# GpSimd makes its score products in four pieces, with output scatters between them

## The chip, the cores and the metric

The program runs on one core of one Trainium2 chip. The core has engines that run their own instruction streams and meet only at semaphores: TensorE (PE, matmuls), VectorE (DVE, elementwise work and reductions), ScalarE (ACT, activations and copies), GpSimd (POOL, elementwise work and the indirect DMAs that scatter rows), and SyncE (SP), which issues most other DMAs. The metric is the device time of one execution in microseconds (us), as the median of the runs taken.

## The reference

Two transformer layers on x of 32 batches x 256 tokens x 128 channels, float32. Cut to what is computed:

```python
x = L0_attn_x                       # (32, 256, 128)
xn = layernorm(x)
x = x + attn0(xn) + moe0(xn)
xn = layernorm(x)
x = x + conv1(xn) + moe1(xn)

# attn0: 16 heads of width 8; attention runs over the HEADS of one token, not over the tokens
q = xn @ Wq + bq ; kv = (xn @ Wdown + bdown) @ Wup + bup ; q, k = rope(q), rope(k)
att = softmax(einsum('bthd,btgd->bthg', q, k) / sqrt(8))     # a 16x16 matrix per token
out = einsum('bthg,btgd->bthd', att, v) @ Wout + bout

# moe0, moe1: 8 experts of width 512, each token takes its best 2 (GELU between two matmuls)
# conv1: layernorm, projection to 3 x 128, two causal convolutions of 128 taps, gates, projection
```

The rotation of q and k is the same for all heads of a token and cancels in the product of a token's own q and k; the kernel leaves it out of the arithmetic.

## The kernel before

The 8192 tokens are 64 tiles of 128 tokens, one token per partition. Attention takes them in 32 pairs, `NPAIR`. Since a token attends only over its own heads, the scores are no matmul: for each pair, somebody multiplies q (broadcast over the key heads) with k (broadcast over the query heads), 2 tiles x 16 x 16 x 8 = 4096 products per partition, and a reduction adds each group of 8. Then the softmax over 16, a second product with v, a second reduction, and a division.

VectorE does this in a loop over the pairs b. `scores(b)` makes or awaits the products, reduces them (L983), takes the maximum (L985) and subtracts it (L986). `weighted(b - 1)` then sums the exponentials of the pair before (L995), multiplies them with v in four instructions (L1000), takes reciprocals (L1007), reduces (L1009) and scales (L1012); `add_heads(b - 3)` adds a finished projection to x (L991). For pairs 0 to 10, VectorE makes the products itself (`own_product`). From pair `OWN` = 11 on, GpSimd makes them (L257, called from its own program), one tile of the pair per instruction, into one of two buffers.

Alongside, from step `T_FIRST` = 10 on, the first layer's experts run: 71 tiles of 256 rows sorted by expert, three in each step. TensorE computes a tile's hidden layer (L678) and output (L691), ScalarE applies the GELU (L486) and evacuates the row indices (L494) and the output (L495), and GpSimd scatters the output to DRAM by row index, two indirect DMAs per tile (L427, `scatter_outputs`). The output buffers are four: ScalarE's evacuation of tile f waits until the scatter of tile f - 4 has landed. ScalarE also evacuates the q, k and v of coming pairs (L501) and takes the exponentials (L510).

The order of the work is written out by hand: every engine walks the same step number b, and counts on semaphores hold the steps together. The ones around the change are:

- `s_on` (heads_ready): VectorE's L1012 of a pair is done. GpSimd waits for it before the first product of a pair: at step b, which makes pair b + 1, for pair b - 2.
- `s_pv` (values_weighted): the fourth L1000 is done. GpSimd waits for it before the second product: at step b, for the L1000 that VectorE runs in its own iteration b.
- `s_qkv` (qkv_ready): q, k and v of the pair are in SBUF.
- `s_pp` (pool_product_halves): counts up by two for each pair; VectorE's L983 of the pair waits for both.
- `s_yev` (expert_out_ready): ScalarE has evacuated a tile; its scatter waits for it. GpSimd scatters three tiles behind (`late`).

Of the kernel before, what the change touches and what calls it, by code (L numbers as in the profile page):

```python
# [8 lines left out]
H, DH = 16, 8  # L9
# [27 lines left out]
NPAIR = NT // 2  # L37
# [6 lines left out]
def tiles_of(b):  # L44

    f0 = PER_STEP * (b - T_FIRST)
    return [f for f in range(max(f0, 0), min(f0 + PER_STEP, NF))] if b >= T_FIRST else []
# [5 lines left out]
def mixed_layers(nc, x, consts, w128, w32, rows, moe0, bout0, moe1, bout1, kpad0, kpad1, out):  # L53
# [5 lines left out]
    with ctx:  # L59
# [3 lines left out]
        def sem(name):  # L63
            return ctx.enter_context(nc.semaphore(name))
# [145 lines left out]
        s_pp = sem("pool_product_halves")  # L210
# [36 lines left out]
        def wait(eng, s, n):  # L247

            if n > 0:
                eng.wait_ge(s, n)  # L250

        def qk_product(eng, b, t, h0=0, n=H):

            q = qkv[:, b % 4, t, h0 * DH:(h0 + n) * DH].rearrange("p (h e) -> p h e", h=n)
            k = qkv[:, b % 4, t, D:2 * D].rearrange("p (g e) -> p g e", g=H)
            o = t * 2048 + h0 * D
            return eng.tensor_tensor(  # L257
                prod[:, b % 2, o:o + n * D].rearrange("p (h g e) -> p h g e", h=n, g=H),
                q[:, :, None, :].to_broadcast([P, n, H, DH]), k[:, None, :, :].to_broadcast([P, n, H, DH]), ALU.mult)
# [116 lines left out]
        @block.gpsimd  # L376
        def _(pool):
            psteps = [0]

            def plink(ins):  # L380
                psteps[0] += 1
                ins.then_inc(s_pst, 1)
                pool.wait_ge(s_pst, psteps[0])

            def in_three_parts(dst, src, n):
                m1 = cst[0:3, C_M1:C_M1 + 1].to_broadcast([3, n])
                m2 = cst[0:3, C_M2:C_M2 + 1].to_broadcast([3, n])
                plink(pool.tensor_copy(partb[:, 0:n], src))
                plink(pool.tensor_tensor(parts[:, 0:n], partb[:, 0:n], m1, ALU.mult))
                plink(pool.tensor_tensor(part[:, 0:n], parts[:, 0:n], src, ALU.add))  # L390
                plink(pool.tensor_copy(partb[:, 0:n], part[:, 0:n]))
                plink(pool.tensor_tensor(parts[:, 0:n], partb[:, 0:n], m2, ALU.mult))
                plink(pool.tensor_tensor(part[:, 0:n], parts[:, 0:n], part[:, 0:n], ALU.add))
                plink(pool.tensor_copy(dst, part[:, 0:n]))

            plink(pool.memset(pat, 0.0))
            pool.iota(patr[:, :, D].bitcast(u32), [[1, FILL]], base=2 * TOKS, channel_multiplier=FILL).then_inc(s_pat, 1)
            for k in range(2):
                pool.iota(tags[:, k, :], [[2, NT]], base=k, channel_multiplier=2 * NT)
            pool.wait_ge(s_cst, 48)  # L400
            pool.wait_ge(s_set, 1)
            pool.wait_ge(s_brow, 1)
            in_three_parts(b3[0:3, :], brow, B_END)
            pool.sem_inc(s_b3, 1)
            pool.wait_ge(s_bf, 32)
            for layer in range(2):
                in_three_parts(bout3[:, layer, :], boutf[:, layer, :], E * D)
            for layer in range(2):
                pool.dma_start(bo3_d[layer], bout3[:, layer, :]).then_inc(s_bo3st, 16)
            pool.sem_inc(s_bo3, 1)  # L410

            def scatter(layer):
                pool.wait_ge(s_rows, layer + 1)
                pool.wait_ge(s_zf[layer], 16 * NFILL)
                for k in range(2):
                    wait(pool, s_sc, 16 * NT * (2 * layer + k))
                    plink(pool.tensor_copy(XN[:, :, D].bitcast(u32), tags[:, k, :]))  # L417
                    for j in range(NT):
                        pool.indirect_dma_start(  # L419
                            sorted_x[layer], bass.IndirectOffsetOnAxis(ap=idx[:, k, j:j + 1], axis=0),  # L420
                            XN[:, j, :], None).then_inc(s_sc, 16)

            def scatter_outputs(layer, f):
                G = layer * NF + f
                pool.wait_ge(s_yev, G + 1)
                for r in range(FR):
                    pool.indirect_dma_start(  # L427
                        y_d[layer], bass.IndirectOffsetOnAxis(ap=yidx[:, G % 4, r:r + 1], axis=0),
                        ys[:, G % 4, r * D:(r + 1) * D], None).then_inc(s_ysc[G % 4], 16)

            scatter(0)
            for b in range(OWN - 1, LAST_STEP + 1):
                late = [f - 3 for f in tiles_of(b) if f >= 3]
                if b + 1 < NPAIR:
                    pool.wait_ge(s_qkv, 2 * (b + 1) + 2)
                    pool.wait_ge(s_on, b - 1)
                    qk_product(pool, b + 1, 0).then_inc(s_pp, 1)
                for f in late[:2]:
                    scatter_outputs(0, f)
                if b + 1 < NPAIR:  # L440
                    pool.wait_ge(s_pv, b)
                    qk_product(pool, b + 1, 1).then_inc(s_pp, 1)
                for f in late[2:]:
                    scatter_outputs(0, f)
            for f in range(NF - 3, NF):
                scatter_outputs(0, f)

            scatter(1)
            for f in range(NF):
                scatter_outputs(1, f)  # L450
# [730 lines left out]
```

## Time and profile before

| | |
|---|---|
| median of 3 runs | 1376.99 us (1376.89 to 1383.17) |
| profiled execution, its own time | 1375.78 us |
| its span | 1373.8 us |
| PE busy | 958.8 us, 70% of the span, 6400 matmuls |
| DVE busy | 860.7 us, 63%, 1144 instructions |
| ACT busy | 602.6 us, 44% |
| POOL busy | 812.7 us, 59%, 617 instructions |
| POOL L257, score products | x42, 189.8 us, mean 4519 ns |
| POOL L427, output scatters, both layers | x284, 309.9 us, mean 1091 ns |
| mean granted TensorE clock | 0.877 |

No engine is busy for the whole span, since the stages have different limits: VectorE's attention to about 310 us, a stage from there to about 735 us in which the rest of attention and the first experts run together, then combination, projection and convolution, and the second experts from about 1035 us. The change touches the stage from 314 to 700 us only. In a chain or a timeline a row gives the start in us from the start of the span, the duration in us, the engine and the line of the program.

### The profile page before, as it was taken

How to read it: one execution, taken by the hardware profiler on the slowest of the kernel's cores; microseconds unless marked ns; L12 is line 12 of the kernel's file. 1: busy time of each engine (PE TensorE's matmuls, PEld its weight loads, DVE VectorE, ACT ScalarE, POOL GpSimd, SP SyncE). 2: the span in 40 equal slices, each digit the busy share in tenths (PEclk: the TensorE clock that was granted, in tenths of full speed). 3: DMA queues.
4: the chain of work that ended last, by engine and by line, in shares of the span. 5: the costliest groups of instructions: out<-in, count | busy, mean ns of one | idle time of the engine just before them, and what ended most of it. 6: DMA issues, size and time to landing. Idle time of an engine off the chain costs nothing.

```text
span 1373.8 us, 19050 instructions
## 1 busy us (share of the span) xinstructions
PE 958.8 (70%) x6400; PEld 843.1 (61%) x6400; DVE 860.7 (63%) x1144; ACT 602.6 (44%) x1533; POOL 812.7 (59%) x617
## 2 busy tenths in 40 slices
PE   1442222217988888887872458889978999999975
PEld 1431011106877776676772457789977999998864
DVE  7949999999999999999995986111122000000028
ACT  0120000005765665565664448900005566665567
POOL 4604877776999999999971003767643445544420
PEclk9995555558999999999996789999998999999988
DMA  5472323313544444544454420189995777777647
GB/s 173 160 294 92 112 79 112 109 42 86 172 131 141 135 138 140 145 132 136 131 160 197 153 93 24 54 277 318 306 355 153 202 201 205 205 206 200 196 186 214
DMA packets 119953, 225.60 MB, mean 164 GB/s; under 512 B 16709, under 2 KB 80101, under 8 KB 117810
## 3 DMA queue, kind: packets, MB, share of 16 engines
q1 hardware_dynamic: 102164, 188.16, 44.9%
q0 software_dynamic: 17344, 35.57, 7.1%
q8 instruction: 52, 0.85, 0.3%
q10 hardware_dynamic: 350, 0.67, 0.2%
q14 instruction: 43, 0.35, 0.1%
HBM read 157.19 MB, written 67.14 MB: 163 GB/s over the span
## 4 chain that ended last, share of the span: by engine, by line
DVE 32%; PE 29%; POOL 15%; DMA 12%; ACT 6%; issue 5%; SPq 1%; POOLq 0%; ACTq 0%; DVEq 0%
PE ps L691 9%; PE ps L678 9%; POOL BG L257 9%; POOL y_tok L427 7%; DVE BG L983 5%; DVE BG L1009 5%; DVE BG L1000 5%; DMA FF<-sorted_x 4%; DMA TPB<-in_kpad 4%; DVE BG L257 3%; DVE XN L880 3%; PE ps L790 2%; PE ps L792 2%; DVE stats L850 2%; PE ps L669 1%
## 5 line engine op out<-in xcount | busy, mean ns | idle before, releaser
L427 POOL DMA_INDIRECT y_tok<-FF,yidx x284 | 309.9, 1091 | 212.4 <-ACT FF L495 154.9
L419 POOL DMA_INDIRECT sorted_x<-XN,idx x256 | 274.4, 1072 | 87.1 <-issue 85.7
L678 PE MATMUL ps<-FF 128*128 128x256 f32 x1136 | 283.9, 395 | 0.0
L691 PE MATMUL ps<-FF 128*128 128x128 f32 x2272 | 280.2, 277 | 0.0
L691 PEld LDWEIGHTS ps<-FF 128*128 128x128 f32 x2272 | 268.7, 194 | 16.8 <-issue 6.3
L486 ACT ACTIVATE FF<-ps,FF 128x256 f32<-128x256 f32 x568 | 230.4, 479 | 37.1 <-PE ps L678 36.5
L678 PEld LDWEIGHTS ps<-FF 128*128 128x128 f32 x1136 | 214.6, 199 | 25.5
L257 POOL TENSOR_TENSOR BG<-TPB 128x2048 f32<-128x2048 f32 x42 | 189.8, 4519 | 11.1 <-DVE BG L1000 6.8
L1127 DVE TENSOR_TENSOR BG<-BG,ps 128x512 f32<-128x512 f32 x16 | 10.6, 686 | 291.3 <-PE ps L824 291.0
L1000 DVE TENSOR_TENSOR BG<-BG,TPB 128x1024 f32<-128x1024 f32 x128 | 147.8, 1214 | 0.0
L983 DVE TENSOR_REDUCE BG<-BG 128x512 f32<-128x4096 f32 x32 | 141.2, 4411 | 0.4
L1009 DVE TENSOR_REDUCE BG<-BG 128x256 f32<-128x4096 f32 x32 | 139.5, 4358 | 0.0
L478 ACT COPY FF<-ps 128x256 f32<-128x256 f32 x142 | 54.2, 382 | 162.0 <-PE ps L669 161.7
L494 ACT COPY yidx<-FF 128x2 uint32<-128x2 uint32 x142 | 27.9, 196 | 221.6 <-PE ps L691 116.8
L417 POOL COPY XN<-tags 128x64 uint32<-128x64 uint32 x4 | 1.2, 298 | 176.4 <-DVEq L962 170.4
L651 PE MATMUL ps<-cst,XN 128*128 128x128 f32 x128 | 24.9, 331 | 89.2 <-DVE XN L880 89.2
L669 PE MATMUL ps<-cst,FF 128*128 128x128 f32 x284 | 56.4, 281 | 43.0 <-DMA FF<-sorted_x 41.4
L719 PE MATMUL ps<-b,ones 128*128 128x384 bf16 x64 | 24.2, 379 | 84.9 <-ACT BG L506 58.5
L790 PE MATMUL ps<-BG,TPB 128*128 128x128 f32 (+1 forms) x352 | 73.0, 289 | 8.9 <-DMA TPB<-in_kpad 7.1
L651 PEld LDWEIGHTS ps<-cst,XN 128*128 128x128 f32 x128 | 19.0, 174 | 91.9 <-DVE XN L880 69.3
L501 ACT COPY TPB<-ps 128x384 f32<-128x384 f32 x64 | 30.8, 481 | 96.7 <-PE ps L720 62.0
L719 PEld LDWEIGHTS ps<-b,ones 128*128 128x128 bf16 x64 | 6.6, 104 | 98.3 <-issue 65.5
(180 smaller groups left out, 1676.8 us busy)
## 6 DMA issues: line engine op xcount, KB each, us to landing
FF<-in_moe SPq DMA_DIRECT2D x142, 514.0 KB
TPB<-in_kpad SPq DMA_DIRECT2D x22, 1024.0 KB, 7.9
sorted_x<-TPB SPq DMA_DIRECT2D x36, 516.0 KB, 4.1
FF<-sorted_x SPq DMA_DIRECT2D x142, 129.0 KB
FF<-in_kpad SPq DMA_DIRECT2D x10, 1024.0 KB, 8.0
BG<-y_tok SPq DMA_DIRECT2D x8, 1024.0 KB, 6.6
X<-y_tok SPq DMA_DIRECT2D x8, 1024.0 KB, 5.9
y_tok<-FF,yidx POOLq DMA_INDIRECT x284, 3.3
```

Of the source, the lines that this page charges most:

```text
L257: return eng.tensor_tensor(prod[:, b % 2, o:o + n * D].rearrange("p (h g e) -> p h g e", h=n, g=H), q[:, :, None, :].to_broadcast([P, n, H ...
L419: pool.indirect_dma_start(sorted_x[layer], bass.IndirectOffsetOnAxis(ap=idx[:, k, j:j + 1], axis=0), XN[:, j, :], None).then_inc(s_sc, 16)
L427: pool.indirect_dma_start(y_d[layer], bass.IndirectOffsetOnAxis(ap=yidx[:, G % 4, r:r + 1], axis=0), ys[:, G % 4, r * D:(r + 1) * D], None ...
L478: act.copy(xsT[:, G % 2, :], psT[:, 0:FT]).then_inc(s_xsT, 1)
L486: g = act.activation(hT[:, G % 2, m, :], psH[2 * (G % 2) + m // 2][:, (m % 2) * FT:(m % 2 + 1) * FT], ACT.Gelu, bias=wc[:, G % 4, HID + MK ...
L669: t = pe.transpose(psT[:, r * P:(r + 1) * P], xs[:, G % 4, r, 0:D], ident)
L678: t = pe.matmul(psH[2 * (G % 2) + m // 2][:, (m % 2) * FT:(m % 2 + 1) * FT], wc[:, G % 4, m * P:(m + 1) * P], xsT[:, G % 2, :], start=True ...
L691: t = pe.matmul(psY[:, r * P:(r + 1) * P], hT[:, G % 2, m, r * P:(r + 1) * P], wc[:, G % 4, HID + m * D:HID + (m + 1) * D], start=False, s ...
L790: pe.matmul(bank[:, k * NT:k * NT + n0], tp[N % 3][:, k, diag:diag + P], V[:, col:col + n0], start=True, stop=False)
L983: link(dve.tensor_reduce(S[:, b % 2, :], prod[:, b % 2, :].rearrange("p (n d) -> p n d", d=DH), AX.X, ALU.add))
L1000: i = dve.tensor_tensor(prodv[:, o:o + n * D].rearrange("p (h e g) -> p h e g", h=n, e=DH), S[:, b % 2, so:so + n * H].rearrange("p (h g) ...
L1009: reduced = mark(dve.tensor_reduce(O, prodv.rearrange("p (n g) -> p n g", g=H), AX.X, ALU.add))
```

## The change

GpSimd's products for a pair were two instructions, each on all 16 query heads of one tile (2048 products per partition). They become four, each on eight query heads (1024 products per partition), through the arguments `h0` and `n` that `qk_product` already has. The step's three tiles of output scatters were placed two after the first product and one after the second. Now one stands after each of the first three pieces, and the fourth piece comes last. The waits stay: `s_qkv` and `s_on` ahead of the first piece, `s_pv` ahead of the third. `s_pp` is counted up at the second and the fourth piece.

```diff
             for b in range(OWN - 1, LAST_STEP + 1):
                 late = [f - 3 for f in tiles_of(b) if f >= 3]
-                if b + 1 < NPAIR:
+                made = b + 1 < NPAIR
+                if made:
                     pool.wait_ge(s_qkv, 2 * (b + 1) + 2)
                     pool.wait_ge(s_on, b - 1)
-                    qk_product(pool, b + 1, 0).then_inc(s_pp, 1)
-                for f in late[:2]:
+                    qk_product(pool, b + 1, 0, 0, H // 2)
+                for f in late[:1]:
                     scatter_outputs(0, f)
-                if b + 1 < NPAIR:
+                if made:
+                    qk_product(pool, b + 1, 0, H // 2, H // 2).then_inc(s_pp, 1)
+                for f in late[1:2]:
+                    scatter_outputs(0, f)
+                if made:
                     pool.wait_ge(s_pv, b)
-                    qk_product(pool, b + 1, 1).then_inc(s_pp, 1)
+                    qk_product(pool, b + 1, 1, 0, H // 2)
                 for f in late[2:]:
                     scatter_outputs(0, f)
+                if made:
+                    qk_product(pool, b + 1, 1, H // 2, H // 2).then_inc(s_pp, 1)
```

GpSimd's queue in step 12, before. L257 are the products (`BG` holds them, `TPB` holds q and k), L427 the scatters, two to a tile:

```order
L257 TENSOR_TENSOR BG<-TPB 128x2048 [waits heads_ready,qkv_ready]
L427 DMA y_tok<-FF,yidx 17408x128 [waits expert_out_ready]
L427 DMA y_tok<-FF,yidx 17408x128
L427 DMA y_tok<-FF,yidx 17408x128 [waits expert_out_ready]
L427 DMA y_tok<-FF,yidx 17408x128
L257 TENSOR_TENSOR BG<-TPB 128x2048 [waits values_weighted]
L427 DMA y_tok<-FF,yidx 17408x128 [waits expert_out_ready]
L427 DMA y_tok<-FF,yidx 17408x128
```

The same step of the changed kernel:

```order
L257 TENSOR_TENSOR BG<-TPB 128x1024 [waits heads_ready,qkv_ready]
L427 DMA y_tok<-FF,yidx 17408x128 [waits expert_out_ready]
L427 DMA y_tok<-FF,yidx 17408x128
L257 TENSOR_TENSOR BG<-TPB 128x1024
L427 DMA y_tok<-FF,yidx 17408x128 [waits expert_out_ready]
L427 DMA y_tok<-FF,yidx 17408x128
L257 TENSOR_TENSOR BG<-TPB 128x1024 [waits values_weighted]
L427 DMA y_tok<-FF,yidx 17408x128 [waits expert_out_ready]
L427 DMA y_tok<-FF,yidx 17408x128
L257 TENSOR_TENSOR BG<-TPB 128x1024
```

The third tile's scatters stood behind all products of the step; they now stand ahead of the last piece. The second tile's scatters still stand behind the whole of the first tile's products, and the first tile's behind only half of them. VectorE's queue is the same in both kernels; one iteration of it, for reference:

```order
L983 TENSOR_REDUCE BG<-BG 128x512 [waits pool_product_halves]
L985 TENSOR_REDUCE BG<-BG 128x32 [waits vector_step]
L986 TENSOR_TENSOR BG<-BG 128x512 [waits vector_step]
L995 TENSOR_REDUCE BG<-BG 128x32 [waits probs_ready]
L1000 TENSOR_TENSOR BG<-BG,TPB 128x1024 x4
L1007 RECIPROCAL BG<-BG 128x32 [waits vector_step]
L1009 TENSOR_REDUCE BG<-BG 128x256 [waits values_weighted]
L1012 TENSOR_TENSOR BG<-BG 128x256 [waits heads_transposed,vector_step]
L991 TENSOR_TENSOR X<-X,ps 128x256 [waits attention_out_psum]
```

Nothing moved here; the wait of L983 is for the second and the fourth piece now.

## Rows read from the trace of the kernel before

**Rows 1.** Chain that ended last, window 381 to 400 us, shares by line

```profile
by line: POOL BG L257 71.4%; POOL y_tok L427 40.4%; issue 12.8%
```

**Rows 2.** Timeline of POOL, same window; start us, us, instruction, idle before it

```profile
381.14 4.53 POOL L257 TENSOR_TENSOR BG<-TPB 128x2048 f32<-128x2048 f32 x1
385.84 1.00 POOL L427 DMA_INDIRECT y_tok<-FF,yidx  x1 [0.17 <-issue]
...
388.13 4.51 POOL L257 TENSOR_TENSOR BG<-TPB 128x2048 f32<-128x2048 f32 x1
392.81 1.27 POOL L427 DMA_INDIRECT y_tok<-FF,yidx  x1 [0.17 <-issue]
394.39 1.39 POOL L427 DMA_INDIRECT y_tok<-FF,yidx  x1 [0.30 <-issue]
396.08 1.96 POOL L427 DMA_INDIRECT y_tok<-FF,yidx  x1 [0.30 <-issue]
...
399.33 4.53 POOL L257 TENSOR_TENSOR BG<-TPB 128x2048 f32<-128x2048 f32 x1
```

**Rows 3.** Busy time by stretch: start:end, length, engines, PEclk, DMA share, GB/s

```profile
344.78:526.51 181.73, 153.58 (x968) 131.97 (x967) 180.69 (x121) 113.14 (x278) 165.75 (x81) 0.95 0.49 142
690.00:735.00 45.00, 33.89 (x240) 30.08 (x239) 32.51 (x26) 24.76 (x66) 29.71 (x25) 1.00 0.43 128
```

**Rows 4.** Timeline of DVE, window 381 to 400 us

```profile
384.73 1.23 DVE L1012 TENSOR_TENSOR BG<-BG 128x256 f32<-128x256 f32 x1
...
386.22 4.41 DVE L983 TENSOR_REDUCE BG<-BG 128x512 f32<-128x4096 f32 x1
...
391.38 1.82 DVE L986 TENSOR_TENSOR BG<-BG 128x512 f32<-128x512 f32 x1
393.13 0.67 DVE L995 TENSOR_REDUCE BG<-BG 128x32 f32<-128x512 f32 x1
393.72 4.61 DVE L1000 TENSOR_TENSOR BG<-BG,TPB 128x1024 f32<-128x1024 f32 x4
398.26 0.34 DVE L1007 RECIPROCAL BG<-BG 128x32 f32<-128x32 f32 x1
```

**Rows 5.** Timeline of DVE, 300 to 320 us, POOL not multiplying beside these

```profile
304.65 0.35 DVE L1007 RECIPROCAL BG<-BG 128x32 f32<-128x32 f32 x1
...
309.31 0.42 DVE L1012 TENSOR_TENSOR BG<-BG 128x256 f32<-128x256 f32 x1
...
309.99 4.63 DVE L257 TENSOR_TENSOR BG<-TPB 128x1024 f32<-128x1024 f32 x4
...
319.82 0.69 DVE L986 TENSOR_TENSOR BG<-BG 128x512 f32<-128x512 f32 x1
```

**Rows 6.** Groups by line, POOL: xcount, busy us, mean ns, idle before

```profile
L393 POOL TENSOR_TENSOR BG<-BG 3x1024 f32<-3x1024 f32 x3 | 7.0, 2328 | 0.2
```

**Rows 7.** Timeline of ACT, window 391 to 398 us

```profile
397.26 0.19 ACT L494 COPY yidx<-FF 128x2 uint32<-128x2 uint32 x1 [3.41 <-DMA y_tok<-FF,yidx]
```

**Rows 8.** Timeline of POOL, window 300 to 352 us

```profile
325.73 4.54 POOL L257 TENSOR_TENSOR BG<-TPB 128x2048 f32<-128x2048 f32 x1 [6.78 <-DVE BG L1000]
333.58 4.53 POOL L257 TENSOR_TENSOR BG<-TPB 128x2048 f32<-128x2048 f32 x1 [3.31 <-ACT TPB L501]
```

**Rows 9.** Timeline of DVE, iterations 10, 11, 30 and 31

```profile
325.56 0.35 DVE L1007 RECIPROCAL BG<-BG 128x32 f32<-128x32 f32 x1
...
343.71 0.34 DVE L1007 RECIPROCAL BG<-BG 128x32 f32<-128x32 f32 x1
...
688.93 0.34 DVE L1007 RECIPROCAL BG<-BG 128x32 f32<-128x32 f32 x1
...
695.05 4.41 DVE L983 TENSOR_REDUCE BG<-BG 128x512 f32<-128x4096 f32 x1
```

**Rows 10.** Chain that ended last, window 710 to 716 us

```profile
711.04 0.34 DVE X L991
...
711.52 0.27 PE ps L707
```

## The prediction

> **What bounds the kernel now.** I read the chain of waits first. In the stage that the change touches it alternates between GpSimd's products (L257) and scatters (L427); in one step of it nothing else appears [rows 1]. So I read GpSimd's timeline of that step next. It is closed: product, two scatters, product, four scatters, product, and every gap is 0.02 to 0.30 us with "issue" as its cause [rows 2]. The step from 381.14 to 399.33 takes 18.19 us; the ten steps from 344.78 to 526.51 take 181.73, or 18.17 each [rows 3]. The reader is to see that GpSimd waits for no other engine there.
>
> VectorE's timeline of the same step comes next [rows 4]. It has no gap either (180.69 us busy of 181.73 [rows 3]), but not all of it is work. L986 takes 1.82 us where it takes 0.69 with no product beside it, and L1012 takes 1.23 against 0.42 [rows 4, 5]. The product that started at 388.13 ends at 392.64 and L995 follows the stretched L986 at 393.13, 0.49 later [rows 2, 4]. L983, a reduction with one input, runs beside the same product in 4.41 us and is not held. In the other direction, the scatters that meet the four L1000 take 1.27, 1.39 and 1.96 us against 1.00 [rows 2]. VectorE free of this needs, from one L1007 to the next: 5.34 to the next pair's first instruction (304.65 to 309.99 [rows 5]), 5.16 from L983 to L986, 0.61 for L986 (its 0.69 less the 0.08 by which L995 overlaps it), 0.59 from L995 to L1000, and 4.54 to L1007 [rows 4]: 16.24 us. The engines hold each other up, and 18.17 is GpSimd's sum.
>
> The Trainium skill, page "SBUF — State Buffer", section "SBUF: two separate sides", says that VectorE and GpSimd share a port pair as an exclusive lock, for an operation with two SBUF inputs against a GpSimd operation that reads SBUF, and that whoever starts first keeps it for the whole instruction. The trace agrees: 1.82 against 0.69.
>
> **The change, part by part.** *The pieces.* GpSimd's elements stay the same. The trace has no piece of 1024 such elements. Half of 4.52 is 2.26, which is the lower end; GpSimd's own product of two 1024-element inputs took 2.328 [rows 6], though on three partitions. I take 2.33. For the upper end I add the 0.17 us that GpSimd needs to go from a product to a scatter: 2.50. Queueing a tile's scatters behind a piece costs 2.46 when VectorE reduces (385.67 to 388.13) and 3.14 when it multiplies (392.64 to 395.78) [rows 2].
>
> *The scatters between.* What matters is the wait for `s_pv`, which stands ahead of the third piece as it stood ahead of the second product. Before, it cost nothing: that product started at 399.33, while L1007 had started at 398.26, and a product that really waited started 0.17 after L1007's start (325.56 to 325.73) [rows 8, 9]. So it had 0.90 us in hand. After the wait came one whole product, 4.53, and then VectorE's next L983 could go. Now after the wait come a piece, a tile's scatters, and a piece. I follow one step from L1007's start, calling the pieces 1 to 4:
>
> - Piece 3 starts at 0.17 and ends at 2.50.
> - The third tile's scatters run beside L1009, a reduction: 2.46, to 4.96.
> - Piece 4 wants to start at 4.96. L1012 started at 4.66 (304.65 to 309.31 [rows 5]) and lasts 0.42; I let the piece start at 5.02. It ends at 7.35.
> - VectorE would have reached L983 at 5.34. It waits until 7.45, two microseconds that were not there before (0.10 of them for the signal, an estimate from the 0.17 above, which also held the last L1000's end).
> - Piece 1 of the next step finds `s_on` counted up by the L1012 just named, so it follows at 7.37 and ends at 9.70.
> - The first tile's scatters, beside L983: to 12.16.
> - Piece 2 starts at 12.16. L986 is ready at 7.45 + 5.16 = 12.61, 0.45 too late, and is held until piece 2 ends at 14.49.
> - L995 follows at 14.98 and L1000 at 15.57; L1007 at 20.11.
> - The second tile's scatters, 3.14, end at 17.6 under the L1000 instructions. GpSimd then waits 2.6 us for `s_pv`.
>
> The step is 20.11 us against 18.17: plus 1.94. All four pieces and two tiles' scatters are now in series with L986 to L1000. One tile's scatters have cover and GpSimd pays its own wait instead. What was saved, the scatter that took 1.96 beside L1000, lies in that wait and is worth nothing.
>
> The order of events hardly depends on the 0.45. If L986 got in first at 12.61, piece 2 would follow at 13.2 and end at 15.6, L1000 would wait for it instead of L986, and L1007 would come at 20.2.
>
> *Other queues.* The waits for the scatters' landing are on ScalarE (L494 [rows 7]), 3.41 us there. The first and third tiles' scatters now come earlier in the step relative to VectorE, so these waits shrink. TensorE and ScalarE gain slack and decide nothing. GpSimd's wait for `s_qkv` cost 3.31 once, at 333.58 [rows 8], and never again. Would TensorE's clock fall when a step has 10% more idle time? From 690 to 735 us TensorE was 75% busy and granted 1.00, against 85% and 0.95 in the ten steps [rows 3], so no.
>
> *The sum.* Step 11 starts at 333.58 as before: its first two pieces and two tiles' scatters, 4.66 + 6.28, end at 344.5. Waiting for a running L1000 adds 0.6, so piece 3 starts at 345.1. L1007 of iteration 12 comes at 345.1 + 19.94 = 365.0, against 343.71 + 18.17 = 361.9. Eighteen more steps bring iteration 30 to 365.0 + 18 x 20.11 = 727.0, against 688.93 [rows 9]: 38.1 late. L983 of pair 31 follows 7.45 later, at 734.4 against 695.05: 39.4 late. No products follow. The stage's end hangs on VectorE's L1012 and L991, which release TensorE's last matmuls (L991 at 711.04, L707 at 711.52 [rows 10]), so nothing of the 39.4 is given back, and the later stages shift whole. On the profiled execution's own time, 1375.78 us, this gives 1415.2; that execution lies 1.2 us under the median, which I leave. For pieces of 2.26 the step is 0.28 shorter, times 19 or so: 1410. For 2.50 it is 0.68 longer: 1428.
>
> The Trainium skill, page "GPSIMD Engine Reference", section "3.1 Elementwise — side-by-side cycle accounting", gives about 2.6 cycles for each element of a two-input operation, and the page's clock is 1.2 GHz. By it a piece would be estimated at 2.22 us, the step at 19.67 and the time at 1407. No trace row of this case has the piece itself, so the row of 2.328 decides.
>
> **The rivals.** *Faster: the wait does not bind, and GpSimd stays the bound.* Its own sum would be 4 x 2.33 + 2 x 2.46 + 3.14 + 0.04 = 17.4 against 18.17, over 20 steps -15 us: 1361. For it: GpSimd is the closed chain now [rows 1, 2]. Against it: the wait is in the queue with 0.90 us in hand, and L1000 would have to come 2.7 us earlier than the pieces allow.
>
> *No change: the lock does not bite at L986.* Then VectorE sets the step: 7.45 + 5.16 + 0.61 + 0.59 + 4.54 = 18.35, plus 0.18. Over 19 steps that is 3.4, with 2 us for step 11 and the end: 1381. Against it: in each of the ten steps a product that overlaps L986 stretched it. For it: the overlap hangs on times that my sum gives to within half a microsecond, and some scatters may fall otherwise.
>
> *Much slower: piece 2 loses to L986 and is not let in between the L1000 instructions.* It would start when L1007 does, at 18.35, end at 20.7, and the second tile's scatters would take it to 23.1 before piece 3: a step of 23.0, +4.9 over 20 steps, 1473. It decides from the point where scatters or pieces run 0.45 us longer than I have them. Against it: the scatters of before got in at the ends of single L1000 instructions (the one at 394.39 finished at 395.78, well inside the four [rows 2, 4]), and L995, with one input, leaves a gap first.
>
> **How the numbers follow.** The forecast, 1415 with its own range of 1407 to 1432, has 0.80. The faster rival has 0.08, no change 0.06, much slower 0.06. Together the rivals are the two in ten that the range leaves out; below it I allow for a lock that bites in part of the steps, above it for pieces at 2.50 and an ill-placed scatter: 1397 to 1436. A difference under 0.5%, 6.9 us, could not be told from none. Faster by more than that 0.08, within it 0.06, slower 0.86.
>
> **What would show it.** In the changed kernel's profile: pieces of 2.33 us, steps of 20.1 us on GpSimd's timeline; a wait of 2.6 us ahead of every third piece, released by L1000; a gap of about 2 us on VectorE ahead of L983, released by L257; L986 still stretched, to about 2.5 us; L1012 back at 0.42. The stage from 690 us on should look as before, 39 us later. I am wrong if GpSimd's timeline stays closed, if L983 starts 5.34 after L1007, or if L986 takes 0.69.

## The result and the profile after

The changed kernel is slower: 1428.15 us median of 4 runs (1426.69 to 1428.73) against 1377.41 us (1376.89 to 1383.17) for the kernel before, a ratio of 1.0357 with a 95% interval of 1.0328 to 1.0386. The profiled execution took 1428.73 us, its span is 1426.8 us. A second set of runs gave 1.0313 (1.0295 to 1.0332).

In the changed file VectorE's lines stand seven further down: L983 is L990, L986 is L993, L995 is L1002, L1000 is L1007, L1007 is L1014, L1009 is L1016, L1012 is L1019, L991 is L998. Scatters keep L427 and products L257. From the page of the changed kernel, the chain by engine, the two groups of GpSimd and the reduction of VectorE that awaits the products (line, engine, operation, count, busy us, mean ns, idle before and its releaser):

```profile
DVE 54%; PE 28%; DMA 9%; ACT 4%; issue 2%; POOL 2%; SPq 1%; POOLq 0%; ACTq 0%; DVEq 0%
...
L427 POOL DMA_INDIRECT y_tok<-FF,yidx x284 | 291.2, 1025 | 218.0 <-ACT FF L502 163.8
...
L257 POOL TENSOR_TENSOR BG<-TPB 128x1024 f32<-128x1024 f32 x84 | 197.2, 2349 | 69.0 <-DVE BG L1007 57.0
...
L990 DVE TENSOR_REDUCE BG<-BG 128x512 f32<-128x4096 f32 x32 | 141.2, 4411 | 3.3 <-POOL BG L257 2.9
```

A piece takes 2.349 us. The scatters did get cheaper: 1025 ns on average where they took 1091. But GpSimd now idles 69 us ahead of the products, 57 of them for the fourth L1007, and the chain has left it for VectorE. The prediction had expected VectorE to wait some 2 us ahead of L990 in every step; over the whole kernel it waits 2.9 us there for GpSimd. One step on GpSimd's timeline, which answers to [rows 2]:

```profile
405.92 2.35 POOL L257 TENSOR_TENSOR BG<-TPB 128x1024 f32<-128x1024 f32 x1 [2.66 <-DVE BG L1007]
408.43 1.00 POOL L427 DMA_INDIRECT y_tok<-FF,yidx  x1 [0.16 <-issue]
409.74 0.96 POOL L427 DMA_INDIRECT y_tok<-FF,yidx  x1 [0.30 <-issue]
410.72 2.34 POOL L257 TENSOR_TENSOR BG<-TPB 128x1024 f32<-128x1024 f32 x1
413.50 2.34 POOL L257 TENSOR_TENSOR BG<-TPB 128x1024 f32<-128x1024 f32 x1 [0.44 <-DVE BG L1019]
415.99 1.00 POOL L427 DMA_INDIRECT y_tok<-FF,yidx  x1 [0.16 <-issue]
417.30 0.96 POOL L427 DMA_INDIRECT y_tok<-FF,yidx  x1 [0.30 <-issue]
418.29 2.35 POOL L257 TENSOR_TENSOR BG<-TPB 128x1024 f32<-128x1024 f32 x1
420.80 1.27 POOL L427 DMA_INDIRECT y_tok<-FF,yidx  x1 [0.17 <-issue]
422.38 1.39 POOL L427 DMA_INDIRECT y_tok<-FF,yidx  x1 [0.30 <-issue]
```

The third piece waits 2.66 us for the values; one tile's scatters follow, the fourth piece, and after a new wait of 0.44 us the next step's first piece. VectorE over the same step, which answers to [rows 4]:

```profile
405.76 0.34 DVE L1014 RECIPROCAL BG<-BG 128x32 f32<-128x32 f32 x1
406.02 4.36 DVE L1016 TENSOR_REDUCE BG<-BG 128x256 f32<-128x4096 f32 x1
410.41 2.94 DVE L1019 TENSOR_TENSOR BG<-BG 128x256 f32<-128x256 f32 x1
413.27 0.41 DVE L998 TENSOR_TENSOR X<-X,ps 128x256 f32<-128x256 f32 x1
413.61 4.41 DVE L990 TENSOR_REDUCE BG<-BG 128x512 f32<-128x4096 f32 x1
418.05 0.69 DVE L992 TENSOR_REDUCE BG<-BG 128x32 f32<-128x512 f32 x1
418.77 2.43 DVE L993 TENSOR_TENSOR BG<-BG 128x512 f32<-128x512 f32 x1
421.12 0.67 DVE L1002 TENSOR_REDUCE BG<-BG 128x32 f32<-128x512 f32 x1
421.71 4.61 DVE L1007 TENSOR_TENSOR BG<-BG,TPB 128x1024 f32<-128x1024 f32 x4
426.25 0.34 DVE L1014 RECIPROCAL BG<-BG 128x32 f32<-128x32 f32 x1
```

The step is 20.49 us (405.76 to 426.25). VectorE shows no gap. It is late inside two instructions: L1019 takes 2.94 us where it needs 0.42, and L993 takes 2.43 where it needs 0.69 [rows 5]. Both end shortly after a piece of GpSimd does (pieces end at 413.06 and 420.64). In the steady steps, which are like this one, about 4.25 of the 20.49 us are time in which an instruction of VectorE is recorded as running and is held. The stretch of 18 steps and the end of the stage, as busy time by stretch (same columns as [rows 3]):

```profile
364.73:733.65 368.92, 283.91 (x1710) 246.67 (x1710) 367.05 (x217) 199.69 (x488) 287.46 (x180) 0.92 0.41 123
...
738.00:783.00 45.00, 33.25 (x220) 30.49 (x220) 30.95 (x26) 18.58 (x51) 25.30 (x24) 0.88 0.36 108
```

The steps are 368.92 / 18 = 20.50 us each. TensorE was granted 0.92 in them and 0.88 in the end of the stage; [rows 3] has 0.95 and 1.00.

### The profile page after: what moved, and what is told of

Read it like the earlier page. It is cut to its first block, busy times and chain, and to the rows that moved or that the text cites. A ratio compares the mean times of both kernels' runs of the same rounds, so it can differ in the third digit from the quotient of the medians.

```text
span 1426.8 us, 19092 instructions
## 1 busy us (share of the span) xinstructions
PE 976.5 (68%) x6400; PEld 864.8 (61%) x6400; DVE 904.5 (63%) x1144; ACT 601.7 (42%) x1533; POOL 801.5 (56%) x659
## 4 chain that ended last, share of the span: by engine, by line
DVE 54%; PE 28%; DMA 9%; ACT 4%; issue 2%; POOL 2%; SPq 1%; POOLq 0%; ACTq 0%; DVEq 0%
DVE BG L1007 9%; DVE BG L990 9%; DVE BG L1016 9%; PE ps L698 9%; PE ps L685 9%; DVE BG L1019 4%; DVE BG L993 4%; DVE BG L257 3%; PE ps L797 3%; DVE XN L887 3%; DMA FF<-sorted_x 3%; DMA TPB<-in_kpad 2%; PE ps L799 2%; DVE stats L857 2%; DVE BG L992 1%
## 5 line engine op out<-in xcount | busy, mean ns | idle before, releaser
L427 POOL DMA_INDIRECT y_tok<-FF,yidx x284 | 291.2, 1025 | 218.0 <-ACT FF L502 163.8
L698 PEld LDWEIGHTS ps<-FF 128*128 128x128 f32 x2272 | 284.7, 204 | 17.1 <-issue 4.5
L698 PE MATMUL ps<-FF 128*128 128x128 f32 x2272 | 294.7, 286 | 0.0
L685 PE MATMUL ps<-FF 128*128 128x256 f32 x1136 | 271.6, 382 | 0.0
L257 POOL TENSOR_TENSOR BG<-TPB 128x1024 f32<-128x1024 f32 x84 | 197.2, 2349 | 69.0 <-DVE BG L1007 57.0
L685 PEld LDWEIGHTS ps<-FF 128*128 128x128 f32 x1136 | 206.9, 192 | 22.7
L1007 DVE TENSOR_TENSOR BG<-BG,TPB 128x1024 f32<-128x1024 f32 x128 | 149.9, 1231 | 0.0
L990 DVE TENSOR_REDUCE BG<-BG 128x512 f32<-128x4096 f32 x32 | 141.2, 4411 | 3.3 <-POOL BG L257 2.9
L1016 DVE TENSOR_REDUCE BG<-BG 128x256 f32<-128x4096 f32 x32 | 139.5, 4358 | 0.0
L714 PE MATMUL ps<-b,ones 128*128 128x256 bf16 x32 | 11.4, 355 | 128.4 <-DVE X L998 127.8
L714 PEld LDWEIGHTS ps<-b,ones 128*128 128x128 bf16 x32 | 3.3, 104 | 147.1 <-issue 145.9
L658 PEld LDWEIGHTS ps<-cst,XN 128*128 128x128 f32 x128 | 20.5, 185 | 88.3 <-DVE XN L887 65.6
```

What stands on the lines that cost most here:

```text
L257: return eng.tensor_tensor(prod[:, b % 2, o:o + n * D].rearrange("p (h g e) -> p h g e", h=n, g=H), q[:, :, None, :].to_broadcast([P, n, H ...
L427: pool.indirect_dma_start(y_d[layer], bass.IndirectOffsetOnAxis(ap=yidx[:, G % 4, r:r + 1], axis=0), ys[:, G % 4, r * D:(r + 1) * D], None ...
L685: t = pe.matmul(psH[2 * (G % 2) + m // 2][:, (m % 2) * FT:(m % 2 + 1) * FT], wc[:, G % 4, m * P:(m + 1) * P], xsT[:, G % 2, :], start=True ...
L698: t = pe.matmul(psY[:, r * P:(r + 1) * P], hT[:, G % 2, m, r * P:(r + 1) * P], wc[:, G % 4, HID + m * D:HID + (m + 1) * D], start=False, s ...
L990: link(dve.tensor_reduce(S[:, b % 2, :], prod[:, b % 2, :].rearrange("p (n d) -> p n d", d=DH), AX.X, ALU.add))
L1007: i = dve.tensor_tensor(prodv[:, o:o + n * D].rearrange("p (h e g) -> p h e g", h=n, e=DH), S[:, b % 2, so:so + n * H].rearrange("p (h g) ...
```

## The experiments

The columns of the comparison are the same throughout: the median and the ratio to the kernel before on the same chip with its 95% interval; the step, from one reciprocal of VectorE to the next in the profile; and by how much VectorE's two-input instructions ran over what they take alone, the subtraction (L986 before) first and the scaling of the heads (L1012) or the products with the values (L1000) second. Edits of a "changed" or "split" kernel and of the one with the old order are shown against the changed kernel, the others against the kernel before.

| kernel | median us | ratio, 95% | step us | VectorE held, us in a step |
|---|---|---|---|---|
| before | 1377.4 | 1 | 18.17 | 1.13 + 0.80 |
| changed | 1428.2 | 1.0357 (1.0328 to 1.0386) | 20.49 | 1.74 + 2.51 |
| pieces, old order | 1383.0 | 1.0037 (1.0019 to 1.0054) | 18.46 | 1.28 + 0.94 |
| second tile split | 1392.2 | 1.0115 (1.0090 to 1.0139) | 18.77 | 2.52, scaling |
| first tile split | 1391.7 | 1.0113 (1.0089 to 1.0137) | 18.83 | 2.59, value products |
| changed, no values wait | 1422.1 | 1.0336 (1.0310 to 1.0363) | 20.13 | 1.74 + 2.15 |
| changed, piece 4 after heads | 1419.7 | 1.0318 (1.0294 to 1.0342) | 20.21 | 1.77, and a wait of 2.12 |
| before, no values wait | 1376.0 | 1.0000 (0.9984 to 1.0016) | 18.17 | 1.13 + 0.80 |
| before, VectorE takes 4 heads | 1357.1 | 0.9877 (0.9842 to 0.9912) | 17.10 | 0.08 + 0.05 |
| before, VectorE takes 5 heads | 1356.5 | 0.9838 (0.9820 to 0.9856) | 17.14 | 0.04 |
| before, VectorE takes 6 heads | 1361.7 | 0.9902 (0.9868 to 0.9935) | 17.28 | 0.05 |
| changed, again | 1422.6 | 1.0313 (1.0295 to 1.0332) | 20.49 | as changed |

The last column accounts for the one before it. VectorE's own work in a step was 16.24 us in the prediction's sum. Adding what held it gives 16.24 + 1.93 = 18.17, 16.24 + 4.25 = 20.49, 16.24 + 2.22 = 18.46, + 2.52 = 18.76, + 2.59 = 18.83, + 3.89 = 20.13. For piece 4 after the heads it gives 16.24 + 1.77 + 2.12 = 20.13, 0.08 short of the step. This is bookkeeping: it must come out for any engine without gaps, and says where the time is, not why. The reasons come from the single runs.

**Pieces without a new order.** Four pieces, scatters where they stood.

```diff
                     qk_product(pool, b + 1, 0, 0, H // 2)
-                for f in late[:1]:
-                    scatter_outputs(0, f)
-                if made:
                     qk_product(pool, b + 1, 0, H // 2, H // 2).then_inc(s_pp, 1)
-                for f in late[1:2]:
+                for f in late[:2]:
                     scatter_outputs(0, f)
                 if made:
                     pool.wait_ge(s_pv, b)
                     qk_product(pool, b + 1, 1, 0, H // 2)
+                    qk_product(pool, b + 1, 1, H // 2, H // 2).then_inc(s_pp, 1)
                 for f in late[2:]:
                     scatter_outputs(0, f)
-                if made:
-                    qk_product(pool, b + 1, 1, H // 2, H // 2).then_inc(s_pp, 1)
```

> Four pieces of eight heads, but each pair of pieces back to back and all scatters where they stood before. My theory: what costs is the scatters between pieces that the next VectorE reduction waits for, not the number of pieces. Then only the two extra instructions count: 4 x 2.35 against 9.04 us, step 18.17 + 0.36 = 18.5 us, and 19 steps of it 7 us: 1384. Rival, the pieces themselves cost it (dispatch, a further lock for each): step 20.5 us and 1428.

Measured 1383.0 us and a step of 18.46. The number of pieces costs 0.29 us a step. That is their surplus: in this run the two pairs of pieces take 4.67 and 4.65 us, together 9.32, where the two whole products take 9.04 [rows 2]. The rest of the loss, 20.49 less 18.46, is the order.

**Only the second tile split.** The first tile's product is whole, followed by two tiles' scatters; behind the wait come piece, scatters, piece.

```diff
                     pool.wait_ge(s_qkv, 2 * (b + 1) + 2)
                     pool.wait_ge(s_on, b - 1)
-                    qk_product(pool, b + 1, 0, 0, H // 2)
-                for f in late[:1]:
+                    qk_product(pool, b + 1, 0).then_inc(s_pp, 1)
+                for f in late[:2]:
                     scatter_outputs(0, f)
-                if made:
-                    qk_product(pool, b + 1, 0, H // 2, H // 2).then_inc(s_pp, 1)
-                for f in late[1:2]:
-                    scatter_outputs(0, f)
```

> Only the second tile's product is split, with the third tile's scatters between its two pieces; the first tile's product is whole and followed by two tiles of scatters. My theory: the path from the wait for the values is piece, scatters, piece, whole product, and GpSimd then still has four scatters beside L1000, 6.5 us: step 18.75 to 18.95 us, +0.7 x 19.5 = 14 us, 1391; VectorE's L1012 stretched to 2.9 us. Rival, this split alone is the whole cost (it alone lies between the wait and the reduction that needs it): step 20.5, 1428.

Measured 1392.2 us. VectorE's timeline (the reciprocal is L1010, the scaling of the heads L1015, the subtraction L989 here), and the two waits of GpSimd in that step:

```profile
400.50 0.34 DVE L1010 RECIPROCAL BG<-BG 128x32 f32<-128x32 f32 x1
...
405.16 2.96 DVE L1015 TENSOR_TENSOR BG<-BG 128x256 f32<-128x256 f32 x1
...
413.54 0.69 DVE L989 TENSOR_TENSOR BG<-BG 128x512 f32<-128x512 f32 x1
...
419.28 0.34 DVE L1010 RECIPROCAL BG<-BG 128x32 f32<-128x32 f32 x1
```

```profile
400.67 2.35 POOL L257 TENSOR_TENSOR BG<-TPB 128x1024 f32<-128x1024 f32 x1 [0.39 <-DVE BG L1003]
...
408.26 4.53 POOL L257 TENSOR_TENSOR BG<-TPB 128x2048 f32<-128x2048 f32 x1 [0.43 <-DVE BG L1015]
```

This step is 18.78. The whole hold is on the scaling, 2.96 us against the 2.9 forecast, and the subtraction is free. The size of the step came as forecast, but not quite by the path that the expectation names: GpSimd waits 0.39 us for the values and 0.43 for the heads, so its own queue does not set the step. VectorE does, with its own 16.24 us and the 2.5 by which piece, scatters and piece behind the wait for the values hold its scaling. The rival's 20.5 is excluded.

**Only the first tile split.**

```diff
                     pool.wait_ge(s_pv, b)
-                    qk_product(pool, b + 1, 1, 0, H // 2)
+                    qk_product(pool, b + 1, 1).then_inc(s_pp, 1)
                 for f in late[2:]:
                     scatter_outputs(0, f)
-                if made:
-                    qk_product(pool, b + 1, 1, H // 2, H // 2).then_inc(s_pp, 1)
```

> Only the first tile's product is split, with the first tile's scatters between its pieces and the second's behind; the second tile's product is whole, followed by the third tile's scatters. My theory: the path is 0.17 + 4.53 + 2.46 + 2.35 + 2.46 + 2.35 + 5.62 = 19.95 us, +1.8 x 19.5 = 35 us, 1412, with L986 (the subtraction) stretched by a late second piece. Rival, only the split of the second tile costs: step 18.2 to 18.5, 1377 to 1384.

Measured 1391.7 us, between the two theories, and both were wrong. Below are GpSimd's second piece, then VectorE's products with the values (L1005 here), all four and the first by itself:

```profile
412.67 2.35 POOL L257 TENSOR_TENSOR BG<-TPB 128x1024 f32<-128x1024 f32 x1
```

```profile
412.31 7.20 DVE L1005 TENSOR_TENSOR BG<-BG,TPB 128x1024 f32<-128x1024 f32 x4
```

```profile
412.31 3.80 DVE L1005 TENSOR_TENSOR BG<-BG,TPB 128x1024 f32<-128x1024 f32 x1
```

My path had the piece hold the subtraction. With the second product whole, the reduction of the products is not late, so the subtraction and the sum are through when piece 2 comes, and it holds the value products instead. The path is shorter by those two, 0.61 + 0.59: 19.95 - 1.20 = 18.75, measured 18.83.

So the two splits cost 0.60 and 0.66 us alone and 2.32 together. The missing 1.06 comes from the same pair of instructions: the split of the second tile makes VectorE late, and so moves the subtraction and the sum, 1.20 us, behind piece 2, which the split of the first tile has already made late. The 0.14 that this is too much is mostly that the second tile's split adds 0.49 us ahead of piece 1 here, and not 0.60: 7.58 against 7.09 us from the start of piece 3, or of the whole product, to the start of piece 1.

**The wait taken out.**

```diff
                 if made:
-                    pool.wait_ge(s_pv, b)
                     qk_product(pool, b + 1, 1, 0, H // 2)
```

> The changed kernel without GpSimd's wait for the fourth L1000 ahead of the third piece; its buffer is free by the wait for the heads. My theory: that wait puts four pieces and two tiles of scatters in series with L986 to L1000. Without it GpSimd need not stand 2.6 us idle per step and its own sum is 17.4 us; the pieces will now meet L1000, so I give the step 18.5 us, 1384 (between 17.4 and 19.5 us, 1362 to 1403). Rival, the port lock costs the same wherever the pieces fall, and the wait only hid it: step 20.5 or more, 1428 or more.

Measured 1422.1 us: my 1384 was wrong and the rival nearly right. VectorE (L992 is the subtraction, L1006 the value products), then GpSimd's third piece and the next step's first:

```profile
398.52 2.43 DVE L992 TENSOR_TENSOR BG<-BG 128x512 f32<-128x512 f32 x1
...
401.48 6.76 DVE L1006 TENSOR_TENSOR BG<-BG,TPB 128x1024 f32<-128x1024 f32 x4
```

```profile
403.55 2.47 POOL L257 TENSOR_TENSOR BG<-TPB 128x1024 f32<-128x1024 f32 x1
...
413.38 2.34 POOL L257 TENSOR_TENSOR BG<-TPB 128x1024 f32<-128x1024 f32 x1 [1.77 <-DVE BG L1018]
```

The third piece now cuts in among the value products and holds them for 2.15 us (6.76 against 4.61), where with the wait the fourth had held the scaling for 2.51. GpSimd's idle time moved to the wait for the heads, 1.77 us. The wait for the values is worth 0.36 us a step in the profile, not the 2 us that I had put on it; the time alone cannot be told from that of the changed kernel, since the intervals overlap.

**The fourth piece behind the heads.**

```diff
                 if made:
+                    pool.wait_ge(s_on, b)
                     qk_product(pool, b + 1, 1, H // 2, H // 2).then_inc(s_pp, 1)
```

> The changed kernel with one wait more: GpSimd's fourth piece waits for VectorE's scaling of the heads in the same iteration. In the changed kernel that scaling starts 0.31 us ahead of the fourth piece's recorded start and yet is held until the piece ends (2.94 us), which delays the next first piece and the next reduction. My theory: a product behind a scatter takes the port before its recorded start, so the order that the prediction assumed needs this wait; the scaling takes 0.42 again, the step falls from 20.49 to 20.2 us, the time by 19.5 x 0.3 = 6 us to 1422. Rival, something else holds the scaling or the wait costs as much as it saves: step 20.5 or more, 1428 or more.

Measured 1419.7 us (1.0318 against 1.0357 and 1.0313 for the changed kernel), step 20.21. The step agrees with the theory. The 6 us in the time are too few to tell from the changed kernel: the intervals overlap with both of its own. GpSimd, then VectorE:

```profile
410.25 4.64 POOL L257 TENSOR_TENSOR BG<-TPB 128x1024 f32<-128x1024 f32 x2 [0.23 <-DVE BG L1020]
```

```profile
409.75 0.42 DVE L1020 TENSOR_TENSOR BG<-BG 128x256 f32<-128x256 f32 x1
...
412.62 4.42 DVE L991 TENSOR_REDUCE BG<-BG 128x512 f32<-128x4096 f32 x1 [2.12 <-POOL BG L257]
```

This is the order that the prediction had assumed: scaling in 0.42 us, then piece 4 and the next piece 1 without a gap, and VectorE waiting 2.12 us in the open ahead of its reduction. The prediction gave this order a step of 20.11; the added wait keeps piece 4 back by 0.23 us.

**The wait taken out of the kernel before.**

```diff
                 if b + 1 < NPAIR:
-                    pool.wait_ge(s_pv, b)
                     qk_product(pool, b + 1, 1).then_inc(s_pp, 1)
```

> The kernel before, two whole products, without the wait for the values ahead of the second one. My theory: the wait was met 0.9 us before GpSimd came to it, so nothing changes: step 18.17 us, 1377. Rival, the wait sets the phase between the two engines and without it the second product drifts into the L1000 instructions: step above 18.5, above 1384.

Measured 1376.0 us, ratio 1.0000 (0.9984 to 1.0016), step 18.17. In the kernel before, that wait decides nothing once the steps are steady. The first three steps with GpSimd's products differ, 24.36, 16.24 and 17.06 us against 20.91, 18.15 and 18.18, and together they are only 0.4 us longer. The one of 16.24 (reciprocals at 328.17 and 344.40) is a step in which no product holds VectorE: the subtraction takes 0.69 and the scaling 0.43. It measures the sum of 16.24 that the prediction had put together.

**GpSimd relieved.** VectorE multiplies the last 4 (5, 6) query heads of the second tile.

```diff
                     pool.wait_ge(s_pv, b)
-                    qk_product(pool, b + 1, 1).then_inc(s_pp, 1)
+                    qk_product(pool, b + 1, 1, 0, H - 4).then_inc(s_pp, 1)
...
                 else:
+                    dve.wait_ge(s_qkv, 2 * b + 2)
+                    link(qk_product(dve, b, 1, H - 4, 4))
                     dve.wait_ge(s_pp, 2 * (b - OWN) + 2)
```

> The kernel before, with 4 of the 16 query heads of a pair's second tile multiplied by VectorE, just ahead of the reduction, and 12 left to GpSimd. My theory of the kernel before is that GpSimd's own sum is the step, so 1.1 us less of it shortens the step to 17.1 us while VectorE's sum, 16.24 + 0.62, stays under it: 1377.4 - 20 x 1.07 = 1356. Rival, VectorE is the bound that counts: step 18.17 + 0.6, 1389. Second rival, TensorE and ScalarE, which wait for the scatters, take over at 18 us: 1374.

> As the run with 4 heads on VectorE, with 6. GpSimd's sum falls by 1.7 us to 16.5, VectorE's rises to 16.24 + 0.91 = 17.15 and should now set the step, with little of it held by products: 17.2 us, 1377.4 - 20 x 0.97 = 1358. Rival, GpSimd's sum still sets it: 16.6 us, 1346. Second rival, VectorE is held by products as much as before: 19.1 us, 1396.

> The kernel before with 5 of the second tile's 16 query heads on VectorE. With 4 the step was GpSimd's closed sum, 17.10 us; with 6 it was VectorE's, 17.28. My theory: with 5, GpSimd's sum is 16.83 and VectorE's 16.24 + 0.80 + 0.05 = 17.09, so the step is 17.1 us and the time that of 4 heads, 1357. Rival, the two lock each other in a phase that neither 4 nor 6 has, L986 and L1012 both stretched: 17.6 us or more, 1366 or more.

Measured 1357.1, 1361.7 and 1356.5 us, steps 17.10, 17.28 and 17.14. With 4 heads on VectorE (L988 is the subtraction, L1014 the scaling) and GpSimd's shorter product:

```profile
405.09 0.77 DVE L988 TENSOR_TENSOR BG<-BG 128x512 f32<-128x512 f32 x1
...
415.57 0.47 DVE L1014 TENSOR_TENSOR BG<-BG 128x256 f32<-128x256 f32 x1
...
416.30 0.68 DVE L257 TENSOR_TENSOR BG<-TPB 128x512 f32<-128x512 f32 x1
```

```profile
411.98 3.44 POOL L257 TENSOR_TENSOR BG<-TPB 128x1536 f32<-128x1536 f32 x1
```

The times of all three came within 4 us of their forecasts, and GpSimd's sum is confirmed as what set the step before. VectorE got more work and its step became shorter, since the products now come earlier against it. The shorter one ends at 415.42, before the scaling starts; the whole one ends at 405.31, 0.22 after the subtraction's start. Of the 1.93 us of hold 0.13 is left. These versions are faster than both kernels, by 1.0 to 1.6% against the one before.

**The changed kernel again.**

> The changed kernel once more, unaltered. In its first profile the stages between the first combination and the second layer's experts took 308.8 us, where the eight profiles of the kernel before and its variants other than this one took 300 to 304. My theory: nothing there belongs to the change, and TensorE's granted clock in the convolution (0.96 against 1.00) made the difference in that execution; a second profile shows 300 to 304 again, steps of 20.49 us and a time near 1424. Rival, the later start of that stage brings the lower clock each time: 308 again, 1428.

Measured 1422.6 us on a chip where the kernel before took 1378.5, steps of 20.49 again. The convolution's stretch in the first profile and in this one:

```profile
950.00:1078.00 128.00, 117.75 (x993) 116.56 (x992) 22.13 (x32) 0.00 (x0) 78.84 (x83) 0.96 0.94 306
```

```profile
950.00:1078.00 128.00, 114.15 (x995) 112.32 (x994) 22.14 (x32) 0.00 (x0) 78.99 (x84) 0.99 0.98 321
```

From the first combination to the second layer's experts this profile took 302.8 us, not 308.8. The surplus of the first profile is not a constant part of the change. Whether the lower granted clock (0.96) or the slower transfers (306 against 321 GB/s) made it, these runs do not separate.

## Why the prediction was right, and where its sizes were off

The direction held, and in the steady steps the chain of instructions that the prediction followed ran as it said but for one place. The time was 1428 where 1415 was forecast, inside the range. The profiled executions differ by 52.95 us, and 39.4 were forecast. The prediction's upper case, pieces of 2.50 us, also gives 1428; that is chance, for the pieces took 2.35 and other terms made the difference. What the prediction had wrong is the share of the single parts in the loss.

- *GpSimd's closed sum bounds the kernel before.* Right: 1.1 us less of GpSimd's work took 1.07 us off the step.
- *The pieces.* Taken at 2.33, measured 2.349 on average; in the step shown the four take 9.38 where 9.32 was assumed. The estimate of 2.22 from the page "GPSIMD Engine Reference" of the Trainium skill (section 3.1) was too low by 0.13; the row of the three-partition product was the better guide.
- *The wait for the values costs 2.6 us of GpSimd's time, and one tile's scatters have cover.* Right as described: 2.66. As a cause I made too much of it: "what matters is the wait", says the prediction, and without it the step is still 20.13. Of the 2.32 us it accounts for 0.36, the number of pieces for 0.29. The rest is that a piece, made late by scatters, holds VectorE at one place or at another, with the wait or without it.
- *Piece 2 meets L986.* Right: piece 2 begins 12.53 us after the reciprocal (12.16 forecast) and holds the subtraction, recorded from 13.01 (12.61 forecast), for 2.43 us against "about 2.5". It takes both a late VectorE and a late piece 2, as the two half-changes showed.
- *L1012 comes ahead of piece 4 and VectorE waits in the open.* Wrong, and this is the term that was mis-sized: the scaling was put down at 0.42 us and took 2.94. It starts at 4.65 as forecast, and piece 4 at 4.96, when the prediction has it ready, yet the scaling is held until the piece is through. There is no open wait ahead of the reduction in these steps. L990 starts at 7.85 instead of 7.45, and the next first piece, which waits for the scaling, at 7.74 instead of 7.37. These 0.37 us carry through to the end of the step: 20.49 for 20.11. Forcing the assumed order gave 20.21. Over the stage this is 7.0 us: L990 of pair 31 is 46.4 us late (39.4 forecast).
- *Step 11.* Its result was right: the reciprocal of iteration 12 came at 364.74, 365.0 forecast. Its inside was not: piece 2 got in among the value products after 0.12 us, where 0.6 was allowed, and then held them, 6.77 us for 4.62, which the sum left out. That cost nothing, since in the kernel before the whole product held the subtraction of that iteration (2.59 for 0.69), and its reciprocal comes at 343.7 in both kernels.

```profile
339.07 2.48 POOL L257 TENSOR_TENSOR BG<-TPB 128x1024 f32<-128x1024 f32 x1
```

```profile
337.00 6.77 DVE L1007 TENSOR_TENSOR BG<-BG,TPB 128x1024 f32<-128x1024 f32 x4
```

- *Nothing is given back or added behind the stage.* Nearly. The first load of the combination, in the changed kernel and in the one before, from the chains:

```profile
781.37 4.89 DMA BG<-y_tok
```

```profile
733.30 4.75 DMA BG<-y_tok
```

  That is 48.1 late, so 1.6 came at the stage's end. The remaining 4.9 us lie in later stages; in the repeat, where the first combination starts at 781.76, 1.7 remain, so most of them come and go.
- *TensorE's clock would not fall.* Wrong. In the steps it was granted 0.92 where the kernel before had 0.95, with TensorE busy 77% of the time instead of 85%. From 738 to 783 us it was granted 0.88 where [rows 3] has 1.00, at nearly the same 74% busy, and the repeat shows 0.88 again. In the steps this costs nothing that the chain shows, since VectorE sets them; whether it made the 1.6 us at the stage's end, no run separates.

```profile
738.00:783.00 45.00, 33.11 (x220) 30.40 (x220) 31.34 (x26) 18.61 (x51) 25.74 (x24) 0.88 0.35 108
```

- *The rivals.* The faster one needed a wait that does not bind; it bound for 2.66 us in every step, and even without it the step was 20.13 and not 17.4. The one of no change needed an unheld L986, which was held for 1.74. The much slower one needed a piece to be kept out by the four value products. The subtraction did not even get in first: it was recorded 0.48 us behind piece 2. And in step 11 here, and in every step of the kernel with the first tile split and of the one without the values wait, a piece that met the value products got in within one instruction.

## What to carry to other kernels

Where two engines hold each other up, count for each of them its own work in a step plus the time in which it is held, and look for the holds inside durations: a held instruction shows as busy here and the timeline shows no gap. Cutting an operation into pieces with other work between made each piece late by what was put in front of it, and the two late pieces together cost more than the sum of each (2.32 against 0.60 and 0.66). Where such a pair of engines is nearly balanced, try moving a little work from the one whose queue is closed to the other; here it shortened the step of both, from 18.17 to 17.10.

## What the runs showed of the hardware

The recorded starts do not tell which engine will be held. A two-input instruction of VectorE that was recorded 0.31 us ahead of a product of GpSimd (410.41 against 410.72, changed kernel) was held until the product's end. So was one recorded 0.36 us ahead (412.31 against 412.67, first tile split, 3.80 us instead of 1.21). One that had started some 0.9 us ahead was not: in the kernel without the wait the product at 403.55 took 2.47 us, 0.12 longer than a piece takes elsewhere, and the value product in progress was finished first. These two value products took 2.35 us, their time when nothing holds them:

```profile
401.48 2.35 DVE L1006 TENSOR_TENSOR BG<-BG,TPB 128x1024 f32<-128x1024 f32 x2
```

All three products stood right behind a scatter. Either such a product has the port before its recorded start, or VectorE's instruction takes it only some time after its own; no run tells the two apart, and none has a product that starts from a semaphore at such a distance. The rule of "SBUF — State Buffer" in the Trainium skill, that whoever starts first keeps the port for the whole instruction, fits all three if the real starts differ from the recorded ones in this way. The skill's page "GPSIMD Engine Reference", section "2.1 Instruction dispatch", says that a GpSimd core begins the next instruction as soon as its own share of the last is done. That would fit the first reading, but no run here shows it.
